# Keys and values of a cross-attention layer projected first, as seven block products, with attention by head group behind them

## The chip, the cores and the metric

The kernel runs on one core of a Trainium2 chip. The metric is the device time of one execution in microseconds; before the change the median of three runs was 1871.52 us (1866.82 to 1872.19).

## The reference

```python
x = x + tanh(g_xattn) * attn(layernorm(x), ctx)      # x: 8 x 100 x 1024, ctx: 8 x 361 x 1024
x = x + tanh(g_ffn) * experts(layernorm(x))
# attn(latents, context): 32 heads in 8 groups of 4, head size 128
kv = concatenate([context, latents])                 # 461 rows for each of 8 batches
q = rms_norm(latents @ Wq) * q_norm_w                # 1024 x 4096
k = rms_norm(kv @ Wk) * k_norm_w;  v = kv @ Wv       # each 1024 x 1024
out = softmax(q @ k.T / sqrt(128)) @ v, then @ Wo    # 4096 x 1024
# experts: 8 of rank 16, two chosen for each row
```

## The kernel before

Every large product is made to fp32 accuracy by splitting both operands into a rounded part (hi, written by ScalarE) and the rest (lo, subtracted by VectorE); `three` then issues hi times hi, hi times lo and lo times hi.

The order of the work is one hand-written program for each engine, tied together by semaphores; all DMAs are issued by SyncE.

1. Latents are normalised, transposed and split. Queries: 32 heads in two halves of 400 columns, 24 matmuls of 128x400 each. Their squares are summed over the head by TensorE (L615, L616: two matmuls of 128x400 for each half head), the sums turned by eight transposes for each group (L622), scaled by VectorE and raised to the power -0.5 by GpSimd (`group_rms`, L547). Queries go to internal DRAM.
2. Sixteen stages, one for each half of the key and value heads and each batch, with four slots. In a slot TensorE projects one tile of keys and values of the next stage (`proj_chunk`, 48 matmuls of 128x512: 8 blocks of the hidden size, keys and values, three each; a tile has 121, 120, 120 or 100 rows) and, between these, attention for one unit of four heads: `turn_keys`, `scores`, and for the unit before `turn_probs` and `values`. VectorE takes the maximum (L1351), the negated scale and the reciprocal, and multiplies the probabilities (`scale`, L1363); ScalarE takes the exponential (L1039). The key norm's power is on GpSimd (`key_rms`).
3. The output projection in 32 chunks of 4 heads, `chunk_head` being 12 matmuls of 128x400. The first eight run in the last stage beside attention (from 1470 us). From 1586 us on only the other 24 run, and then the small expert layer.

Where an instruction waits, all behind it on its engine wait too. The probabilities of a unit are turned after the next unit's first scores:

```python
scores(u, 0)                      # waits for kT_lo_done, q_lo_done
turn_probs(u - 1, par, t)         # t == 0 waits for p_done, 4 * u + 4 of that unit
```

## Time and profile before

| | us |
|---|---|
| time, median of 3 runs | 1871.52 |
| span of the profiled execution | 1867.1 |
| TensorE busy | 1803.3 (97%) |
| VectorE busy | 1099.9 (59%) |
| ScalarE busy | 846.7 (45%) |
| GpSimd busy | 152.0 (8%) |
| moved by DMA | 169.76 MB, 91 GB/s |

The profile gives the span from first to last instruction of one execution. Its own time outside that span is not shown; the span is 4.4 us under the median. Durations of matmuls overlap, since one starts before the other has drained: what a matmul costs a busy TensorE is the distance from its start to the next start. Busy time counts overlapping instructions once.

### The profile page before, as it was taken

The numbers are of one execution on the slowest core, as the hardware profiler recorded it, in microseconds if no ns is written. First come the engines' busy times: TensorE is split into PE (matmuls) and PEld (weight loads), VectorE is DVE, ScalarE is ACT, GpSimd is POOL, SyncE is SP. The second block draws the span as 40 slices with busy tenths as digits, with TensorE's granted clock in tenths as the row PEclk, the third lists the DMA queues.
The fourth block names the chain that finished last, engine by engine and source line by source line (L and its number), as shares of the span: only waits on it lengthen the run. The fifth ranks groups of instructions, "written<-read, shape, count | busy, mean of one in ns | idle before, by whom it ended". The sixth has DMA issues, their size and how long they took to land.

```text
span 1867.1 us, 26857 instructions
## 1 busy us (share of the span) xinstructions
PE 1803.3 (97%) x9512; PEld 1597.7 (86%) x9512; DVE 1099.9 (59%) x2308; ACT 846.7 (45%) x1594; POOL 152.0 (8%) x176
## 2 busy tenths in 40 slices
PE   5999999999999999999899999999999899999996
PEld 4999999878888888888688888888888789999994
DVE  6533333246666666666766666666666576455556
ACT  4433333235455555555655555554554455433321
POOL 3012111210000000000000000000000000000000
PEclk9999999999999999999999999999999999999999
DMA  6522232301111111111311111111111244656522
GB/s 208 184 99 80 84 133 80 121 21 57 40 57 46 50 56 37 59 52 41 107 57 53 44 57 39 56 56 39 56 41 63 98 178 166 237 186 222 212 98 62
DMA packets 62825, 169.76 MB, mean 91 GB/s; under 512 B 5808, under 2 KB 38576, under 8 KB 57616
## 3 DMA queue, kind: packets, MB, share of 16 engines
q1 hardware_dynamic: 62736, 168.69, 26.9%
q8 instruction: 42, 0.69, 0.2%
q14 instruction: 47, 0.39, 0.1%
HBM read 135.90 MB, written 32.77 MB: 90 GB/s over the span
## 4 chain that ended last, share of the span: by engine, by line
PE 91%; DVE 5%; ACT 2%; issue 1%; DMA 1%; POOL 0%; DVEq 0%; SPq 0%; ACTq 0%
PE bank L579 27%; PE bank L580 27%; PE bank L581 27%; PE bank L724 5%; PE bank L701 1%; PE bank L888 1%; PE bank L616 1%; PE bank L615 1%; DVE wo_lo L1328 0%; DMA w_raw<-Wkv 0%; ACT wo_hi L1016 0%; DMA xa<-x 0%; PE bank L622 0%; DVE at_lo L1333 0%; DVE w_lo L1237 0%
## 5 line engine op out<-in xcount | busy, mean ns | idle before, releaser
L579 PE MATMUL bank<-w_hi,kv_hi 128*128 128x512 f32 x1024 | 422.7, 413 | 2.6 <-DVE w_lo L1237 2.6
L580 PE MATMUL bank<-w_lo,kv_hi 128*128 128x512 f32 x1024 | 403.7, 394 | 0.0
L581 PE MATMUL bank<-w_hi,kv_lo 128*128 128x512 f32 x1024 | 403.7, 394 | 0.0
L1039 ACT ACTIVATE pr<-bank,nm,rqs 100x461 f32<-100x461 f32 x256 | 188.9, 738 | 417.8 <-DVE nm L1356 417.7
L1345 DVE TENSOR_TENSOR pT_lo<-bank,pT_hi 121x400 fp32r<-121x400 f32 x252 | 144.1, 572 | 169.5 <-ACT pT_hi L1032 169.5
L581 PEld LDWEIGHTS bank<-w_hi,kv_lo 128*128 128x128 f32 x1024 | 192.5, 188 | 44.2
L1351 DVE TENSOR_REDUCE mx<-bank 100x1 f32<-100x461 f32 x256 | 162.3, 634 | 114.9 <-PE bank L581 110.9
L579 PEld LDWEIGHTS bank<-w_hi,kv_hi 128*128 128x128 f32 x1024 | 193.1, 189 | 32.4 <-issue 1.7
L580 PEld LDWEIGHTS bank<-w_lo,kv_hi 128*128 128x128 f32 x1024 | 193.4, 189 | 29.9
L579 PE MATMUL bank<-at_hi,wo_hi 128*128 128x400 f32 x512 | 183.0, 357 | 9.2 <-DVE at_lo L1333 6.5
L579 PE MATMUL bank<-xT_hi,wq_hi 128*128 128x400 f32 x512 | 178.0, 348 | 2.4 <-DVE xT_lo L1212 2.4
L581 PE MATMUL bank<-at_hi,wo_lo 128*128 128x400 f32 x512 | 178.6, 349 | 0.0
L580 PE MATMUL bank<-at_lo,wo_hi 128*128 128x400 f32 x512 | 178.6, 349 | 0.0
L580 PE MATMUL bank<-xT_lo,wq_hi 128*128 128x400 f32 x512 | 177.7, 347 | 0.0
L581 PE MATMUL bank<-xT_hi,wq_lo 128*128 128x400 f32 x512 | 177.0, 346 | 0.0
L1032 ACT ACTIVATE pT_hi<-bank 121x400 fp32r<-121x400 f32 x252 | 125.3, 498 | 75.2 <-PE bank L724 75.2
L1264 DVE TENSOR_TENSOR sq_lo<-sq,sq_hi 128x400 fp32r<-128x400 f32 x64 | 36.8, 575 | 172.0 <-ACT sq_hi L980 172.0
L724 PE MATMUL bank<-ident,pr 100*120 100x100 f32 (+2 forms) x1024 | 134.5, 253 | 0.0
L724 PEld LDWEIGHTS bank<-ident,pr 100*120 100x120 f32 (+2 forms) x1024 | 116.8, 147 | 15.2
L1363 DVE TENSOR_SCALAR pr<-pr,rr 100x461 f32<-100x461 f32 x256 | 117.9, 461 | 9.1
L976 ACT ACTIVATE sq<-bank 128x400 f32<-128x400 f32 x64 | 32.3, 505 | 198.6 <-PE bank L581 198.6
L1328 DVE TENSOR_TENSOR wo_lo<-wo_raw,wo_hi 128x2048 fp32r<-128x2048 f32 x32 | 73.1, 2284 | 63.9 <-ACT wo_hi L1016 63.5
(128 smaller groups left out, 3059.6 us busy)
## 6 DMA issues: line engine op xcount, KB each, us to landing
wo_raw<-Wo SPq DMA_DIRECT2D x32, 1024.0 KB, 4.9
at_raw<-at_d SPq DMA_DIRECT2D x32, 800.0 KB, 6.8
wq_raw<-Wq SPq DMA_DIRECT2D x32, 512.0 KB, 6.6
kv_raw<-ctxT SPq DMA_DIRECT2D x32, 480.0 KB, 3.6
q_d<-qo SPq DMA_DIRECT2D x8, 1600.0 KB, 6.2
q_raw<-q_d SPq DMA_DIRECT2D x64, 200.0 KB, 2.4
at_d<-ao SPq DMA_DIRECT2D x64, 200.0 KB, 1.9
kv_raw<-ctxT SPq DMA_DIRECT2D x16, 484.0 KB, 3.6
```

Source lines behind the costliest of these rows:

```text
L579: pe.matmul(o, lh, rh, start=start, stop=False)
L580: pe.matmul(o, lh, rl, start=False, stop=False)
L581: return pe.matmul(o, ll, rh, start=False, stop=stop)
L724: mm = pe.transpose(ps[ptbank(t, last)][0:ROWS[t], i * NQ:(i + 1) * NQ], pr[0:NQ, par, i, OFF[t]:OFF[t] + ROWS[t]], ident[0:NQ, 0:NQ])
L976: act.activation(sq[:], ps[2 * (i % 2) + th][:, 0:TW], ACT.Square).then_inc(sq_done, 1)
L1032: act.activation(pT_hi[0:ROWS[t], t], ps[ptbank(t, not project)][0:ROWS[t], 0:QW], ACT.Copy).then_inc(pT_hi_done, 1)
L1039: act.activation(pr[0:NQ, j % 2, i], ps[sbank(i, not project)][0:NQ, 0:NK], ACT.Exp, bias=nm[0:NQ, i:i + 1], scale=rqs[0:NQ, i:i + 1], acc ...
L1264: dve.tensor_tensor(sq_lo[:, th], sq[:], sq_hi[:], ALU.subtract).then_inc(sq_lo_done, 1)
L1328: dve.tensor_tensor(wo_lo[:, k], wo_raw[k][:], wo_hi[:, k], ALU.subtract).then_inc(wo_lo_done, 1)
L1345: dve.tensor_tensor(pT_lo[0:ROWS[t], t], ps[ptbank(t, not project)][0:ROWS[t], 0:QW], pT_hi[0:ROWS[t], t], ALU.subtract).then_inc(pT_lo_do ...
L1351: dve.tensor_reduce(mx[0:NQ, i:i + 1], ps[sbank(i, not project)][0:NQ, 0:NK], AX.X, ALU.max).then_inc(mx_done, 1)
L1363: dve.tensor_scalar(pr[0:NQ, j % 2, i], pr[0:NQ, j % 2, i], rr[0:NQ, i:i + 1], None, ALU.mult).then_inc(p_done, 1)
```

## The change

Keys and values of all batches come first. The rows of four batches (4 x 461 = 1844) are packed into 15 tiles, and the two halves of the batches, the two halves of the hidden size and the pair keys and values make a product of 2x2 blocks, computed as seven block products (`P1` to `P7`) in Strassen's manner: 30 steps (`STEPS`, 15 tiles by two halves of the heads) of seven products with 12 matmuls of 128x512. The sums of inputs are made by GpSimd, the sums of weights by VectorE (first half) and GpSimd (second), the sums of results partly in the bank (`CHAIN`) and partly by VectorE in `cb`. Each step's keys are normalised, turned, split and stored to internal DRAM, as are the values; one buffer `kst` and one `vst` serve all stores. The latents' transposes are spread over eight steps (`X0`).

Then come nine parts of the queries' projection (a part is a half head, `AHEAD`), 55 slots of one attention unit and one part each, with the queries kept in SBUF, and nine slots with the remaining units, in the last eight of which 28 heads of the output projection run. The squares of a query part are summed by eight matmuls with the squares as the stationary operand and two columns of ones. Probabilities are scaled by GpSimd; loops are written out. From the end of the last unit on the program does what it did.

```diff
-                    mm = three(ps[BV if isv else BK][:, 0:KW], kv_hi[:, j, c], kv_lo[:, j, c],
-                               w_hi[:, c, isv * KW:(isv + 1) * KW], w_lo[:, c, isv * KW:(isv + 1) * KW],
-                               c == 0, c == C - 1)
...
-                    dve.tensor_scalar(pr[0:NQ, j % 2, i], pr[0:NQ, j % 2, i], rr[0:NQ, i:i + 1], None,
-                                      ALU.mult).then_inc(p_done, 1)
...
+ROWS_M = TB * NK
+CTX_M = TB * NC
+NT = -(-ROWS_M // P)
+STEPS = HALVES * NT
+MIXED = CTX_M // P
+KC = C // 2
+P1, P2, P6, P5, P7, P3, P4 = range(7)
+RING = 5
+W_ORDER = (P1, P2, P5, P7, P6, P3, P4)
+W_RANK = {o: n for n, o in enumerate(W_ORDER)}
+X0 = 2
+UNITS = G * B
+AHEAD = 9
+QB = 2 * R
+LAST_Q = UNITS - AHEAD
+OUT0 = LAST_Q
+HEADS_AT = {OUT0 + 1 + n: c for n, c in enumerate((3, 3, 4, 3, 4, 3, 4, 4))}
...
+        kT_d = nc.dram_tensor("kT_d", [P, G, 2, 2 * ROWS_M], F32).ap()
+        v_d = nc.dram_tensor("v_d", [2 * ROWS_M, G, 2, HD], F32).ap()
...
+        def a_src(k, o):
+            raw = kvr[:, k % 2]
+            n = cols(k % NT)
+            return {P1: raw[:, 0, 0:KC, 0:n], P2: raw[:, 0, KC:C, 0:n], P4: raw[:, 1, KC:C, 0:n],
+                    P6: st[:, 1, :, 0:n], P5: st[:, 0, :, 0:n], P7: st[:, 2, :, 0:n], P3: st[:, 1, :, 0:n]}[o]
+        def w_src(n):
+            return wr[:, (0, 1, 0, 2, 0, 3, 1)[n]]
...
     @block.sync
...
+            def store_k(k, m):
+                sp.wait_ge(kT_lo_done, 2 * k + m + 1)
+                h, r0, n = k // NT, rows_at(k, m), cols(k % NT)
+                sp.dma_start(kT_d[:, GH * h:GH * h + GH, :, r0:r0 + n].rearrange("p g l r -> p (g l) r"),
+                             kst[:].rearrange("p g l r -> p (g l) r")[:, :, 0:n].bitcast(F32)).then_inc(k_stored, 16)
+            def store_v(k, m):
+                sp.wait_ge(v_lo_done, 2 * k + 2 - m)
+                h, r0, n = k // NT, rows_at(k, m), cols(k % NT)
+                sp.dma_start(v_d[r0:r0 + n, GH * h:GH * h + GH], vst[0:n].bitcast(F32)).then_inc(v_stored, 16)
...
+            sp.dma_start(wr[:, 0], Wkv[0, 0]).then_inc(wr_in[0], 16)
+            load_kv(0)
+            for i in range(1, 4):
+                sp.dma_start(wr[:, i], Wkv[0, i]).then_inc(wr_in[i], 16)
+            sp.dma_start(qkw[:], vecs).then_inc(consts_in, 16)
+            sp.dma_start(rowc[:], rows).then_inc(consts_in, 16)
+            load_kv(1)
...
+                if k + 2 < STEPS:
+                    load_kv(k + 2)
...
+                store_k(k, 0)
...
+                store_v(k, 1)
+            store_v(STEPS - 1, 0)
+            store_k(STEPS - 1, 1)
...
     @block.gpsimd
...
+            def sums(k):
...
+                raw = kvr[:, k % 2, :, :, 0:n]
+                pool.wait_ge(kv_in[k % 2], kv_need(k))
+                if k >= 1:
+                    pool.wait_ge(a_lo_done, 7 * (k - 1) + P5 + 1)
+                pool.tensor_tensor(st[:, 0, :, 0:n], raw[:, 1, 0:KC], raw[:, 1, KC:C], ALU.add).then_inc(s_sum, 1)
+                pool.wait_ge(s_sum, 4 * k + 1)
+                if k >= 1:
+                    pool.wait_ge(a_lo_done, 7 * (k - 1) + P3 + 1)
+                pool.tensor_tensor(st[:, 1, :, 0:n], st[:, 0, :, 0:n], raw[:, 0, 0:KC], ALU.subtract).then_inc(s_sum, 1)
+                pool.tensor_tensor(st[:, 2, :, 0:n], raw[:, 0, 0:KC], raw[:, 1, 0:KC], ALU.subtract).then_inc(s_sum, 1)
+            def last_sum(k):
+                n = cols(k % NT)
+                pool.wait_ge(a_lo_done, 7 * k + P6 + 1)
+                pool.tensor_tensor(st[:, 1, :, 0:n], kvr[:, k % 2, 0, KC:C, 0:n], st[:, 1, :, 0:n],
+                                   ALU.subtract).then_inc(s_sum, 1)
...
+            sums(0)
+            last_sum(0)
+            for k in range(STEPS):
+                if k >= 1:
+                    key_rms(k - 1, 1)
+                if k == NT:
+                    weight_sums(3)
+                if k + 1 < STEPS:
+                    sums(k + 1)
+                if 0 <= k - X0 < B:
+                    latent_rstd(k - X0)
+                if k == NT - 1:
+                    weight_sums(0)
+                key_rms(k, 0)
+                if k == NT - 1:
+                    weight_sums(1)
+                if k + 1 < STEPS:
+                    last_sum(k + 1)
+                if k == NT - 1:
+                    weight_sums(2)
+            key_rms(STEPS - 1, 1)
+            def group_rms(g):
+                pool.wait_ge(ms_done, g + 1)
+                pool.tensor_tensor(rq[0:NQ, g], ms[0:NQ], mhalf[0:NQ], ALU.pow).then_inc(rq_done, 1)
+            def scale(u, i):
+                a = 4 * u + i
+                pool.wait_ge(rr_done, a + 1)
+                pool.tensor_scalar(pr[0:NQ, u % 2, i], pr[0:NQ, u % 2, i], rr[0:NQ, i:i + 1], None,
+                                   ALU.mult).then_inc(p_done, 1)
+            group_rms(0)
+            for u in range(UNITS):
+                for i in range(R):
+                    scale(u, i)
+                    if u % B == B - 1 and i == 0 and u + 1 < UNITS:
+                        group_rms(u // B + 1)
...
     @block.tensor
...
+            def product(k, o, bank, start):
+                h, n, p = k // NT, cols(k % NT), 7 * k + o
+                pe.wait_ge(a_lo_done, p + 1)
+                if k % NT == 0:
+                    pe.wait_ge(w_lo_done, 7 * h + W_RANK[o] + 1)
+                s = p % RING
+                for c in range(KC):
+                    mm = three(ps[bank][0:n, 0:KW], a_hi[:, s, c, 0:n], a_lo[:, s, c, 0:n], w_hi[:, o, c], w_lo[:, o, c],
+                               start and c == 0, c == KC - 1, not start)
+                mm.then_inc(prod_done, 1)
...
+            def step(k):
+                a = CHAIN[k % 2]
+                if k >= 2:
+                    pe.wait_ge(kn_done, 2 * (k - 2) + 2)
+                product(k, P1, a, True)
+                if k >= 1:
+                    pe.wait_ge(c12_done, k)
+                product(k, P2, BK, True)
+                if k >= 1:
+                    turn_keys(k - 1, 1)
+                pe.wait_ge(p1_done, k + 1)
+                product(k, P6, a, False)
+                if k >= 1:
+                    pe.wait_ge(c22_done, k)
+                    pe.wait_ge(c12a_done, k)
+                product(k, P5, CK, True)
+                pe.wait_ge(u2_done, k + 1)
+                product(k, P7, a, False)
+                turn_keys(k, 0)
+                pe.wait_ge(c11_done, k + 1)
+                product(k, P3, BK, True)
+                if 0 <= k - X0 < B:
+                    turn_latents(k - X0)
+                pe.wait_ge(u3_done, k + 1)
+                product(k, P4, a, False)
...
+            def squares(n):
+                g, i, th = n // QB, n // 2 % R, n % 2
+                pe.wait_ge(sq_lo_done, n + 1)
+                if n == 0:
+                    pe.wait_ge(ones_done, 1)
+                    pe.wait_ge(kT_lo_done, 2 * STEPS - 1)
+                if n % QB == 0 and g >= 1:
+                    pe.wait_ge(ms_done, g)
+                for bb in range(TB):
+                    c0 = 2 * (R * (TB * th + bb) + i)
+                    o = ps[SS][0:NQ, c0:c0 + 2]
+                    pe.matmul(o, sq_hi[:, bb * NQ:(bb + 1) * NQ], ones[:], start=True, stop=False)
+                    mm = pe.matmul(o, sq_lo[:, bb * NQ:(bb + 1) * NQ], ones[:], start=False, stop=True)
+                mm.then_inc(ss_done, 1)
...
+            for n in range(AHEAD):
+                for c in range(C):
+                    query_part(n, c)
+                    if n == 0 and c == 1:
+                        turn_keys(STEPS - 1, 1)
+                    if n >= 1 and c == 4:
+                        squares(n - 1)
...
+            def slot(u):
+                n = u + AHEAD if u < LAST_Q else None
+                def c_(c):
+                    if n is not None:
+                        query_part(n, c)
+                scores(u, 0)
+                if u >= 1:
+                    turn_probs(u - 1, 0)
+                c_(0)
+                scores(u, 1)
+                if u >= 1:
+                    turn_probs(u - 1, 1)
+                c_(1)
...
+                c_(3)
+                if u >= 1:
+                    values(u - 1, 2)
+                c_(4)
+                if u + AHEAD - 1 < 2 * H:
+                    squares(u + AHEAD - 1)
+                c_(5)
+                if u >= 1:
+                    values(u - 1, 3)
+                c_(6)
+                c_(7)
...
     @block.scalar
...
+            def values_hi(k, m):
+                v, n = 2 * k + 1 - m, cols(k % NT)
+                if v >= 1:
+                    act.wait_ge(v_stored, 16 * v)
+                act.activation(vst[0:n, :, 0], cb[0:n, 1 + m].rearrange("p (g d) -> p g d", g=GH), ACT.Copy).then_inc(v_hi_done, 1)
...
     @block.vector
...
+            weight_lo(0, 0)
+            operand_lo(0)
+            dve.wait_ge(wr_in[2], 16)
+            weight_sum(0, 2, 0)
+            weight_lo(0, 1)
+            operand_lo(1)
+            dve.wait_ge(wr_in[3], 16)
+            dve.wait_ge(t_done, 1)
+            weight_sum(2, 3, 2)
+            weight_lo(0, 2)
+            dve.wait_ge(w_lo_done, 3)
+            weight_sum(0, 3, 0)
+            operand_lo(2)
+            weight_lo(0, 3)
+            operand_lo(3)
+            weight_lo(0, 4)
+            dve.wait_ge(t_done, 3)
+            weight_sum(1, 1, 0)
...
+            def at_product(k, o):
+                if k == 0 and o == 0:
+                    weight_lo(0, 5)
+                if k == 0 and o == 2:
+                    weight_lo(0, 6)
+                if (k, o) in W_AT:
+                    weight_lo(1, W_AT[k, o])
+                p = 7 * k + o + RING - 1
+                if o == 0 and k >= 1:
+                    key_sums(k - 1, 1)
+                if o == 1 and k >= 1:
+                    normalise_keys(k - 1, 1)
+                if o == 2:
+                    sum_c11(k)
+                if o == 5:
+                    sum_c22(k)
+                    start_c12(k)
+                if o == 6:
+                    sum_c12(k)
+                if o == 4:
+                    normalise_keys(k, 0)
+                if p < 7 * STEPS:
+                    operand_lo(p)
+                if o == 0 and k >= 1:
+                    values_lo(k - 1, 0)
...
+            def mean_squares(g):
+                dve.wait_ge(ss_done, QB * g + QB)
+                if g >= 1:
+                    dve.wait_ge(rq_done, g)
+                dve.tensor_scalar(ms[0:NQ].rearrange("p (n o) -> p n o", o=1),
+                                  ps[SS][0:NQ, 0:2 * B * R].rearrange("p (n o) -> p n o", o=2)[:, :, 0:1],
+                                  1.0 / HD, RMS_EPS, ALU.mult, ALU.add).then_inc(ms_done, 1)
...
+            def slot(u):
+                n = u + AHEAD - 1
+                prev = u >= 1
+                maxima(u, 0)
+                if prev:
+                    p_split(u - 1, 0)
...
+                    p_split(u - 1, 3)
+                inverse(u, 3)
+                if u % B == B - 1 and u + 1 < UNITS:
+                    mean_squares(u // B + 1)
+                if u + 1 < UNITS:
+                    q_split(u + 1)
+                if n < 2 * H:
+                    next_wq(n)
```

## Rows read from the trace of the kernel before

**Rows 1.** the profile's page: engine busy time, and last chain by engine

```profile
PE 1803.3 (97%) x9512; PEld 1597.7 (86%) x9512; DVE 1099.9 (59%) x2308; ACT 846.7 (45%) x1594; POOL 152.0 (8%) x176
...
PE 91%; DVE 5%; ACT 2%; issue 1%; DMA 1%; POOL 0%; DVEq 0%; SPq 0%; ACTq 0%
```

**Rows 2.** stretches of the span: length, busy time of each engine, clock, DMA

```profile
0.00:42.00 42.00, 18.74 (x97) 16.03 (x98) 29.34 (x56) 18.46 (x30) 15.81 (x24) 0.99 0.61 198
...
1470.00:1586.00 116.00, 105.75 (x589) 100.32 (x588) 77.42 (x126) 58.67 (x87) 0.00 (x0) 0.97 0.47 171
1586.00:1867.10 281.10, 260.58 (x1452) 246.96 (x1450) 152.84 (x222) 91.25 (x87) 13.65 (x16) 0.99 0.48 170
```

**Rows 3.** matmuls in order of time, 128x512: start, duration; first and last of 104

```profile
370.72 0.39 PE L580 MATMUL bank<-w_lo,kv_hi 128*128 128x512 f32 x1
...
394.64 0.40 PE L581 MATMUL bank<-w_hi,kv_lo 128*128 128x512 f32 x1
```

**Rows 4.** the last chain in order of time: one period of the queries' loop

```profile
132.63 0.87 PE bank L622 x8
171.42 0.87 PE bank L622 x8
```

**Rows 5.** the last chain in order of time: four key and four probability transposes

```profile
410.27 0.40 PE bank L701 x4
410.68 0.42 PE bank L724 x4
```

**Rows 6.** matmuls in order of time: scores; first of one head and what follows

```profile
903.67 0.37 PE L579 MATMUL bank<-kT_hi,q_hi 128*100 128x462 f32 x1
...
904.30 0.34 PE L579 MATMUL bank<-pT_hi,v_hi 120*128 120x400 f32 x1
```

**Rows 7.** groups by form: count, busy, mean ns of one

```profile
L1431 DVE TENSOR_TENSOR v_lo<-v_raw,v_hi 128x512 fp32r<-128x512 f32 x64 | 43.8, 685 | 0.5 <-ACT v_hi L1103 0.5
...
L1351 DVE TENSOR_REDUCE mx<-bank 100x1 f32<-100x461 f32 x256 | 162.3, 634 | 114.9 <-PE bank L581 110.9
...
L1039 ACT ACTIVATE pr<-bank,nm,rqs 100x461 f32<-100x461 f32 x256 | 188.9, 738 | 417.8 <-DVE nm L1356 417.7
...
L1363 DVE TENSOR_SCALAR pr<-pr,rr 100x461 f32<-100x461 f32 x256 | 117.9, 461 | 9.1
...
L1328 DVE TENSOR_TENSOR wo_lo<-wo_raw,wo_hi 128x2048 fp32r<-128x2048 f32 x32 | 73.1, 2284 | 63.9 <-ACT wo_hi L1016 63.5
...
L1016 ACT ACTIVATE wo_hi<-wo_raw 128x2048 fp32r<-128x2048 f32 x32 | 61.3, 1916 | 108.5 <-PE bank L581 100.9 <-DMA at_raw<-at_d 7.6
```

**Rows 8.** GpSimd and VectorE in order of time, around a group's mean squares

```profile
101.60 5.44 POOL L547 TENSOR_TENSOR rqt<-ms,mhalf 100x32 f32<-100x32 f32 x1 [66.58 <-DVE ms L1249]
...
104.96 0.57 DVE L1264 TENSOR_TENSOR sq_lo<-sq,sq_hi 128x400 fp32r<-128x400 f32 x1 [3.44 <-ACT sq_hi L980]
```

**Rows 9.** GpSimd and VectorE in order of time, in the output projection

```profile
1671.98 2.24 DVE L1328 TENSOR_TENSOR wo_lo<-wo_raw,wo_hi 128x2048 fp32r<-128x2048 f32 x1
...
1672.15 2.12 POOL L570 TENSOR_SCALAR mv<-mv 100x1 f32<-100x1 f32 x1 [205.77 <-DVE mv L1473]
```

**Rows 10.** GpSimd in order of time, at the start

```profile
1.28 0.29 POOL L535 TENSOR_SCALAR_AFFINE_SELECT ident<-ident 128x128 f32<-128x128 f32 x1 [0.24 <-POOL epst L533]
```

**Rows 11.** DMA issues by line: size, median us to landing

```profile
wo_raw<-Wo SPq DMA_DIRECT2D x32, 1024.0 KB, 4.9
...
kv_raw<-ctxT SPq DMA_DIRECT2D x32, 480.0 KB, 3.6
...
at_d<-ao SPq DMA_DIRECT2D x64, 200.0 KB, 1.9
```

**Rows 12.** matmuls in order of time, after a wait in the last slots

```profile
1478.02 0.67 PE L579 MATMUL bank<-at_hi,wo_hi 128*128 128x400 f32 x1 [3.62 <-DVE at_lo L1333]
1478.49 0.54 PE L580 MATMUL bank<-at_lo,wo_hi 128*128 128x400 f32 x1
1478.82 0.54 PE L581 MATMUL bank<-at_hi,wo_lo 128*128 128x400 f32 x1
```

More of the change, by code:

```diff
@@ new lines, in _ @@
+            sums(0)
+            last_sum(0)
+            for k in range(STEPS):
+                if k >= 1:
[15 more added lines that the diff above has]
+                    weight_sums(2)
@@ L594, in _, with three @@
-            pe.wait_ge(pool_consts, 4)
-            for b in range(B):
+            def three(o, lh, ll, rh, rl, start, stop, more=False):
+                pe.matmul(o, lh, rh, start=start, stop=False, skip_group_check=more)
+                pe.matmul(o, lh, rl, start=False, stop=False, skip_group_check=more)
+                return pe.matmul(o, ll, rh, start=False, stop=stop, skip_group_check=more)
+            def product(k, o, bank, start):
[8 more added lines that the diff above has]
+                mm.then_inc(prod_done, 1)
@@ L903, in _ @@
             accumulators_free(0, 1)
-            chunk(0, 1, 0, 0, first=True)
-            chunk(0, 1, 0, 1)
-            with pe.Fori(1, G // 2 - 1) as gp:
-                chunk(0, 1, gp, 0)
-                chunk(0, 1, gp, 1)
-            chunk(0, 1, G // 2 - 1, 0)
-            chunk(0, 1, G // 2 - 1, 1, last=True)
+            for m in range(G, 2 * G):
+                chunk(m)
             for c in range(2 * G):
@@ new lines, in _, with p_split @@
+            ins.then_inc(pad_done, 1)
+            for n in range(AHEAD - 1):
+                copy_queries(n)
+                squares_lo(n)
+                next_wq(n)
+            mean_squares(0)
+            q_split(0)
+            def p_split(u, t):
+                dve.wait_ge(pT_hi_done, 4 * u + t + 1)
+                if t == 0 and u >= 1:
+                    dve.wait_ge(pv_done, u)
+                dve.tensor_tensor(pT_lo[0:ROWS[t], t], ps[ptbank(u, t)][0:ROWS[t], 0:QW],
+                                  pT_hi[0:ROWS[t], t], ALU.subtract).then_inc(pT_lo_done, 1)
@@ L1435, in _ @@
-            for j in range(KT):
-                slot(-1, j, 1, 0, False, True)
-                if j == 0:
-                    mean_squares(G)
-                if j == 2:
-                    keep_rms(G)
-            q_split(0)
-            normalise_keys(0, 0, 0)
-            stages(dve, lambda s, par, half: [slot(s, j, par, half, True, projects(s)) for j in range(GH)])
-            last = 4 * STAGES - 1
+                dve.tensor_tensor(at_lo[:, m % 2], at_raw[:, m % 2], at_hi[:, m % 2], ALU.subtract).then_inc(wo_lo_done, 1)
```

1835 lines of the change are left out of this document (875 added, 960 removed).

## The prediction

> **What bounds the kernel now.** I read the page first: TensorE is busy for 1803.3 of 1867.1 us and makes up 91% of the chain that ended last; VectorE has 59%, ScalarE 45%, GpSimd 8% [rows 1]. Then the stretches, to see where TensorE is idle: 42 − 18.74 = 23.3 us in the first 42 us, 116 − 105.75 = 10.3 us in the last stage beside the output projection, 20.5 us in the 281.1 us after 1586 us [rows 2]. The whole span has 1867.1 − 1803.3 = 63.8 us idle [rows 1], so 43.3 us lie ahead of 1586 us, where all edits are. What comes after is the same program and is kept at 281.1 us. Last the lists in order of time, for what one matmul costs a full queue. Durations mislead there, since they overlap. From 370.72 to 394.64 us there are 103 steps from start to start: 0.2322 us for a 128x512 [rows 3], though its duration is 0.39. A queries' group lasts 38.79 us with 208 matmuls of 128x400 and eight transposes of 0.87 together [rows 4]: 0.1823 us each. Four transposes take 0.40 [rows 5], the three matmuls of a scores' head 904.30 − 903.67 = 0.63 [rows 6].
>
> **What TensorE issues less or more.** (a) Projection: 1024 x 3 = 3072 matmuls become 30 steps x 7 x 12 = 2520 of the same 128x512 form (the tile of 52 rows only has fewer columns in the stationary operand). 552 x 0.2322 = −128.2 us [rows 3]. (b) Squares: 128 matmuls of 128x400 go, −23.3 us [rows 4]; 512 with two moving columns and 100 stationary ones come. No row has this form. A small transpose also has a short stream behind a full load of the stationary operand: 0.87/8 = 0.109 us [rows 4]; the cheapest is 0.35/4 to 0.40/4 [rows 5]; the dear end is a full 0.1823. I take 0.109: +55.7, net +32.4 (bounds +22 and +70). (c) The turned sums go: eight times 0.87, −7.0 us [rows 4]. (d) Key transposes: 64 x 4 become 60 x 4, −0.4 x 4 = −1.6 us [rows 5]. Queries, scores, values, probabilities and output keep their counts. Sum: −104.4 us of work for TensorE. In return it waits where it did not.
>
> **The start.** The first step needs all seven weight blocks. A load of 1024 KB lands after 4.9 us and one of 480 KB after 3.6 [rows 11], so each further MB adds 1.3/544 x 1024 = 2.4 us. The first 1 MB, issued at 0.8, lands at 5.7 and, with tile 0 between, the third weight load at 5.7 + 3 x 2.4 = 13 us. VectorE stands at it, with the second block's lo queued behind; from there seven operations of 2048 columns at 2.28 and three of 512 at 0.69 lie ahead of the third product [rows 7], which starts at 13 + 16 + 2 = 31 us. Behind it come the last weight, two more, and the first key norm (square, sum, power, product) before the sixth product; the step ends near 50 us against 20.4 for a full one: 30 us idle, where the start had 23.3.
>
> **The other 29 steps.** A step is 84 x 0.2322 + 0.9 = 20.4 us for TensorE. VectorE has 19 operations of 512 columns at 0.69, 13 us [rows 7]; it hides if no wait falls wrong. The closest is the one buffer for values: `values_hi` waits for the store before it. That store can start some 0.2 us before the step's end; its 512 KB take between 1.9 (200 KB) and 3.6 to 3.8 us [rows 11]. Then ScalarE and VectorE run 0.63 + 0.69, and the product that normalises the second key block is queued behind, 0.69: done 5.5 us into the next step, when `turn_keys` is due after two products of 2.79. So it nearly hides; the GpSimd sums can push it. I take 0.4 us for each step, 12 us (0 to 60).
>
> **Second half's weights.** Seven subtractions, 16 us of VectorE, and four GpSimd sums of 2048 columns fall on steps 14 and 15. The sums are bounded by VectorE's 2.28 [rows 7] and 16 x 0.29 = 4.6 [rows 10], scaled by columns from 128. The key sums queue behind the subtractions; I take 14 us (4 to 30). **Handover** to the queries: last key norm, 6.5 MB of split latents and the first group's power before the first exponential, 8 us (3 to 15).
>
> **The slots.** A slot: 24 x 0.1823 + 4 x 0.63 + 12 x 0.1823 + 1.5 + 0.9 = 11.5 us, where there were 17.9. VectorE and ScalarE have about 8.5 and 8 us. Fourth scores end 6.6 us into the slot; maximum 0.63 and exponential 0.74 [rows 7], two operations on one column and the reading of the accumulator between them, and the queue ahead of them (the fourth head's own split among it) lead to about 9.3; GpSimd's fourth scaling follows. It is due at 11.5 + 0.6 = 12.1. Bounds for one scaling: VectorE's 0.46 [rows 7] and 0.29 x 461/128 = 1.04 [rows 10]; I take 0.9, nearer the GpSimd row. It hides with 1.9 us to spare, and the slots cost nothing more.
>
> **Group boundaries.** Not hidden. GpSimd raises 32 columns to the power in 5.44 us [rows 8]. Before, that lay beside the queries with nothing behind. Now, in each eighth unit, it is queued after the first scaling and waits for `mean_squares`, which VectorE does only after the fourth reciprocal, at 9.4. So power until 15, three scalings until 17.7, and `turn_probs` due at 12.1 waits 5.5 us. After 3.62 us of idle, matmuls of 128x400 came 0.33 us apart instead of 0.18, which is 1.2 GHz instead of 2.4 (the stretch's granted clock is 0.97) [rows 2, 12]; some ten of them so spaced cost 1.5 us. Six boundaries at 7 us, and one in unit 55, whose slot has no queries to cover it, at 11: 53 us (35 to 65).
>
> **Last slots.** Their wait before was 10.3 us in four slots [rows 2], from weights and heads split behind attention (1.9 + 2.3 us for the weights alone [rows 7]). Eight such slots: 19 us (10 to 35).
>
> **Sum.** New idle 30 + 12 + 14 + 8 + 53 + 19 = 136 us, old 43.3. −104.4 + 136 − 43.3 = −11.7, so a span of 1855.4. The median lies 1871.5 − 1867.1 = 4.4 above the span of before: **1860 us**.
>
> **Rows against a rule.** A GpSimd operation on one element, issued 0.17 us into VectorE's 2.24 us subtraction, took 2.12 us and ended just after it [rows 9]. But VectorE's 0.57 us subtraction ran at its usual length inside GpSimd's 5.44 us power [rows 8]. The Trainium skill (SBUF — State Buffer, section "SBUF: two separate sides") says that the two engines share a port pair which one holds for a whole instruction while the other fully blocks. By that the first row agrees and the second does not; for sums that stream rather than compute no row here decides. The Trainium skill (GPSIMD Engine Reference, section 3.1 on elementwise work) gives 4497 ns for a GpSimd addition of 2048 columns; by it one sum of 512 would be an estimated 1.1 us, against 1.16 by scaling the row.
>
> **Rivals.**
> *R1, boundaries hidden, TensorE stays the bound.* The 53 us vanish if the power is shorter than 5.4 or the profile's VectorE runs ahead; with steps unstalled too: 1860 − 53 − 20 (steps, weights) = 1787. For: TensorE has been 97% busy in a program of the same kind [rows 1]. Against: the order of GpSimd's queue. Chance 0.17.
> *R2, slower: GpSimd's scaling is late in each slot.* It decides from 3 us for the fourth scaling, less if those before wait. VectorE's next subtractions, 0.57 and in every second slot 1.22, may go first, as in the wait of [rows 9]. Each 1 us late costs 62 us over the units: 1922. Chance 0.17.
> *R3, slower: VectorE and GpSimd exclude each other in the steps.* GpSimd has four sums at 1.16 and two powers at 1.2, 7 us, on top of VectorE's 13: 20 of 20.4, and more in the eight steps with latents. If nothing overlaps, order leaves some 2 us for each step and the weights cost 15 more: 1860 + 50 + 15 = 1925. Chance 0.16. This is what the Trainium skill's port rule (SBUF — State Buffer, same section) would do here.
> *The forecast,* 0.5, own range 1825 to 1885.
>
> A difference within 0.3% (5.6 us) can't be told from none. The forecast's half splits into 0.36 faster, 0.10 same, 0.04 slower: faster 0.36 + 0.17 = 0.53; same 0.10; slower 0.04 + 0.17 + 0.16 = 0.37. The range runs from R1 to beyond R2 and R3: 1775 to 1935.
>
> **What would show it.** 2520 matmuls 0.232 apart; the two-column squares 0.11 apart; one step every 20.4 to 21.3 us; the third product at about 31 us; slots of 11.5 to 12; TensorE idle over 4 us only at units 8, 16 to 56, waiting for GpSimd's scaling; 136 + 20.5 = 157 us of idle in all against 63.8. Wrong if steps exceed 22 us, slots exceed 12.3, or the two-column squares cost 0.18.

## The result, and the profile after

The changed kernel takes **1986.55 us** (median of 4 runs, 1984.04 to 1988.65), the kernel before 1871.76 (4 runs, 1866.82 to 1872.19): a ratio of 1.0617, 95% interval 1.0601 to 1.0633. It is 6.2% slower, outside the range of 1775 to 1935.

The page of the changed kernel, profiled at a span of 1983.7 us:

```profile
PE 1748.3 (88%) x9264; PEld 1542.6 (78%) x9264; DVE 1174.7 (59%) x2129; ACT 913.5 (46%) x1680; POOL 713.4 (36%) x548
...
PEclk8998988889999998999989998999897899999998
...
DMA packets 229494, 278.12 MB, mean 140 GB/s; under 512 B 67972, under 2 KB 203972, under 8 KB 223732
...
PE 68%; DMA 11%; DVE 8%; POOL 5%; issue 3%; ACT 3%; SPq 1%; DVEq 0%; ACTq 0%; POOLq 0%
PE bank L654 20%; PE bank L655 19%; PE bank L656 19%; DMA v_d<-vst 7%; PE bank L778 5%; POOL rq L631 2%; DMA kT_d<-kst 2%; POOL pr L636 2%; PE bank L675 2%; PE bank L745 1%; DVE a_lo L1291 1%; PE bank L744 1%; DVE wo_lo L1524 1%; DVE kn L1315 1%; DVE w_lo L1297 1%
```

Against [rows 1], TensorE's share of the last chain fell from 91% to 68%, and DMA went from 1% to 11%: 7% of the span is the store of values. TensorE is idle for 1983.7 − 1748.3 = 235.4 us, where the prediction had 156.5, and busy for 1748.3, where it had 1803.3 − 104.4 = 1698.9. The two differences, 78.9 and 49.4, are the 128.3 us between the predicted span of 1855.4 and this one.

Where it was lost is seen by cutting the span at the work's own marks: the issue of a step's first key store (steps 0, 15, 29), the first scores, the end of TensorE's work ahead of unit 55's first scores, the first copy of an accumulator.

```profile
0.00:51.09 51.09, 25.33 (x78) 19.32 (x79) 39.33 (x30) 22.67 (x24) 19.59 (x18) 0.83 0.37 144
51.09:464.00 412.91, 335.77 (x1443) 266.86 (x1442) 240.25 (x333) 160.87 (x272) 153.43 (x141) 0.89 0.68 152
464.00:748.52 284.52, 281.39 (x1287) 226.12 (x1286) 177.98 (x265) 127.67 (x224) 109.69 (x109) 1.00 0.61 154
748.52:816.55 68.03, 52.79 (x302) 49.95 (x299) 18.27 (x30) 14.22 (x24) 2.47 (x3) 0.87 0.49 158
816.55:1502.20 685.65, 638.20 (x3933) 595.58 (x3931) 452.11 (x1073) 413.64 (x901) 355.11 (x227) 0.96 0.36 109
1502.20:1696.30 194.10, 151.45 (x780) 135.62 (x780) 93.83 (x177) 83.14 (x149) 59.40 (x37) 0.87 0.45 151
1696.30:1983.70 287.40, 263.36 (x1451) 249.18 (x1450) 152.91 (x222) 91.26 (x87) 13.68 (x16) 0.97 0.49 171
```

(Length, then busy time of TensorE, its loads, VectorE, ScalarE and GpSimd, the granted clock, the DMA share and GB/s.) Beside the prediction's terms:

| stretch | predicted | after | more |
|---|---|---|---|
| step 0 | 50 | 51.1 | +1 |
| steps 1 to 15: 15 x 20.8 + 14 | 326 | 412.9 | **+87** |
| steps 16 to 29: 14 x 20.8 | 291 | 284.5 | −7 |
| way to the first scores: 216 x 0.1823, 64 x 0.109, rest of a step 4, idle 8 | 59 | 68.0 | +9 |
| units 0 to 54: 55 x 11.5 + 42 | 675 | 685.7 | +11 |
| units 55 to 63 (what is left of 1855) | 173 | 194.1 | +21 |
| output | 281 | 287.4 | +6 |

Steps 16 to 29 took 20.3 us each at full clock, as forecast; the same program took 27.5 us in steps 1 to 15, at 0.89. Of the 87 us more, 60 lie in steps 1 to 10 (267.9 us for 208), 15 in steps 11 to 13, 12 in the last two. What ScalarE does in step 4, in order of time:

```profile
147.12 12.65 SPq L380 DMA_DIRECT2D v_d<-vst  x2
...
158.06 0.63 ACT L1014 ACTIVATE vst<-cb 128x512 fp32r<-128x512 f32 x1 [8.41 <-DMA v_d<-vst]
158.72 0.69 DVE L1329 TENSOR_TENSOR vst<-cb,vst 128x512 fp32r<-128x512 f32 x1 [8.28 <-ACT vst L1014]
159.33 0.69 DVE L1315 TENSOR_TENSOR kn<-bank,rk 128x512 f32<-128x512 f32 x1
...
160.07 1.12 PE L675 MATMUL bank<-ident,kn 128*128 128x128 f32 x4 [6.14 <-DVE kn L1315]
```

The first value store of the step is issued at 147.12, and the next split of values can begin only at 158.06: the store took 10.9 us to land, and ScalarE, VectorE and TensorE stood behind it in turn, 8.41, 8.28 and 6.14 us. In step 16 the same chain runs so:

```profile
486.50 4.57 SPq L380 DMA_DIRECT2D v_d<-vst  x2
489.35 0.63 ACT L1014 ACTIVATE vst<-cb 128x512 fp32r<-128x512 f32 x1 [1.09 <-DMA v_d<-vst]
490.02 0.69 DVE L1329 TENSOR_TENSOR vst<-cb,vst 128x512 fp32r<-128x512 f32 x1 [0.95 <-ACT vst L1014]
490.62 0.68 DVE L1315 TENSOR_TENSOR kn<-bank,rk 128x512 f32<-128x512 f32 x1
...
492.39 0.60 PE L675 MATMUL bank<-ident,kn 128*128 128x128 f32 x4
```

Here it landed in 2.85 us, and TensorE didn't wait; in steps 16 to 29 it had two waits over 0.4 us, of 1.1 and 0.9. Over the whole program, by the list of waits (total, times, longest):

```profile
ACT vst L1014 <- DMA v_d<-vst: 120.8, 29, 12.5
...
PE bank L675 <- DVE kn L1315: 88.8, 23, 11.3
```

A boundary between groups (unit 7 to 8):

```profile
906.38 0.19 DVE L1468 TENSOR_SCALAR ms<-bank 100x32 f32<-100x32 f32 x1 [0.68 <-PE bank L745]
906.65 5.71 POOL L631 TENSOR_TENSOR rq<-ms,mhalf 100x32 f32<-100x32 f32 x1 [4.25 <-DVE ms L1468]
912.36 4.29 POOL L636 TENSOR_SCALAR pr<-pr,rr 100x461 f32<-100x461 f32 x3
...
916.70 1.14 PE L778 MATMUL bank<-ident,pr 100*121 100x100 f32 x4 [7.41 <-POOL pr L636]
```

This is the queue that was forecast: power, then three scalings, then TensorE. Each scaling takes 1.43 us, not 0.9. From store to store of attention's outputs a slot is 11.37 us, and the six at boundaries are 21.0, 21.8, 20.7, 21.7, 20.6 and 21.7: 9.9 more each, where I had 7.

At unit 55 the prediction had one wait, for the power. It is there, and ahead of it stands another:

```profile
1502.24 0.36 SPq L478 DMA_DIRECT2D wo_raw<-Wo  x1
...
1503.67 0.60 SPq L479 DMA_DIRECT2D at_raw<-at_d  x1
1504.31 0.53 SPq L452 DMA_DIRECT2D kT<-kT_d  x1
...
1515.28 0.70 PE L654 MATMUL bank<-kT,q_hi 128*100 128x462 f32 x1 [13.07 <-DMA kT<-kT_d]
...
1528.46 5.71 POOL L631 TENSOR_TENSOR rq<-ms,mhalf 100x32 f32<-100x32 f32 x1 [6.84 <-DVE ms L1468]
...
1534.16 4.29 POOL L636 TENSOR_SCALAR pr<-pr,rr 100x461 f32<-100x461 f32 x3
...
1538.50 1.14 PE L778 MATMUL bank<-ident,pr 100*121 100x100 f32 x4 [7.81 <-POOL pr L636]
```

SyncE waits for the last query (1502.2) before the output's first two chunks, 3.6 MB, and the load of unit 55's keys stands behind them: 13 us. The power and three scalings then hold TensorE for 7.81 us, as at the other boundaries.

### The profile page after: what moved, and what is told of

It is laid out like the page before. It is cut to its first block, busy times and chain, and to the rows that moved or that the text cites. A ratio compares the mean times of both kernels' runs of the same rounds, so it can differ in the third digit from the quotient of the medians.

```text
span 1983.7 us, 26304 instructions
## 1 busy us (share of the span) xinstructions
PE 1748.3 (88%) x9264; PEld 1542.6 (78%) x9264; DVE 1174.7 (59%) x2129; ACT 913.5 (46%) x1680; POOL 713.4 (36%) x548
## 4 chain that ended last, share of the span: by engine, by line
PE 68%; DMA 11%; DVE 8%; POOL 5%; issue 3%; ACT 3%; SPq 1%; DVEq 0%; ACTq 0%; POOLq 0%
PE bank L654 20%; PE bank L655 19%; PE bank L656 19%; DMA v_d<-vst 7%; PE bank L778 5%; POOL rq L631 2%; DMA kT_d<-kst 2%; POOL pr L636 2%; PE bank L675 2%; PE bank L745 1%; DVE a_lo L1291 1%; PE bank L744 1%; DVE wo_lo L1524 1%; DVE kn L1315 1%; DVE w_lo L1297 1%
## 5 line engine op out<-in xcount | busy, mean ns | idle before, releaser
L636 POOL TENSOR_SCALAR pr<-pr,rr 100x461 f32<-100x461 f32 x256 | 370.2, 1452 | 420.5 <-DVE rr L1520 420.5
L654 PE MATMUL bank<-w_hi,a_hi 128*128 128x512 f32 (+1 forms) x840 | 347.5, 414 | 28.5 <-DVE a_lo L1291 13.9
L655 PE MATMUL bank<-w_lo,a_hi 128*128 128x512 f32 (+1 forms) x840 | 338.9, 403 | 0.0
L656 PE MATMUL bank<-w_hi,a_lo 128*128 128x512 f32 (+1 forms) x840 | 338.1, 403 | 0.0
L1153 ACT ACTIVATE pr<-bank,nm,rq 100x461 f32<-100x461 f32 x256 | 188.7, 737 | 147.2 <-DVE nm L1511 144.4
L654 PEld LDWEIGHTS bank<-w_hi,a_hi 128*128 128x128 f32 (+1 forms) x840 | 162.1, 193 | 67.0 <-issue 21.5
L1144 ACT ACTIVATE pT_hi<-bank 120x400 fp32r<-120x400 f32 (+2 forms) x256 | 129.1, 504 | 144.9 <-PE bank L778 144.9
L1499 DVE TENSOR_TENSOR pT_lo<-bank,pT_hi 120x400 fp32r<-120x400 f32 (+2 forms) x256 | 145.2, 567 | 83.8 <-ACT pT_hi L1144 81.9
L656 PEld LDWEIGHTS bank<-w_hi,a_lo 128*128 128x128 f32 (+1 forms) x840 | 161.1, 192 | 40.5 <-issue 0.6
L778 PE MATMUL bank<-ident,pr 100*120 100x100 f32 (+2 forms) x1024 | 141.9, 262 | 55.7 <-POOL pr L636 55.7
L655 PEld LDWEIGHTS bank<-w_lo,a_hi 128*128 128x128 f32 (+1 forms) x840 | 162.1, 193 | 36.6 <-issue 0.4
```

What stands on the lines that cost most here:

```text
L636: pool.tensor_scalar(pr[0:NQ, u % 2, i], pr[0:NQ, u % 2, i], rr[0:NQ, i:i + 1], None, ALU.mult).then_inc(p_done, 1)
L654: pe.matmul(o, lh, rh, start=start, stop=False, skip_group_check=more)
L655: pe.matmul(o, lh, rl, start=False, stop=False, skip_group_check=more)
L656: return pe.matmul(o, ll, rh, start=False, stop=stop, skip_group_check=more)
L778: mm = pe.transpose(ps[ptbank(u, t)][0:ROWS[t], i * NQ:(i + 1) * NQ], pr[0:NQ, u % 2, i, OFF[t]:OFF[t] + ROWS[t]], ident[0:NQ, 0:NQ])
L1144: act.activation(pT_hi[0:ROWS[t], t], ps[ptbank(u, t)][0:ROWS[t], 0:QW], ACT.Copy).then_inc(pT_hi_done, 1)
```

## Experiments

Each is the changed kernel with one edit, unless it says otherwise. Kernels were run in four sessions, each on one chip: e1 to e4; e0, e5, e6, e8; e10, e11; e12, e13. All but e10 are single runs, beside which the kernel before took 1868.2 to 1872.0 us. "Steps 1 to 10" is a ninth of the time between the first key stores of steps 1 and 10; it was 27.5 us in the changed kernel. Line numbers are each kernel's own.

**e1: the power in two halves.** Of a group's squares only the last part belongs to the second half of the batches, so the first 16 columns can be raised a slot earlier.

```diff
-                    if u % B == B - 1 and i == 0 and u + 1 < UNITS:
-                        group_rms(u // B + 1)
+                if u % B >= B - 2 and u // B + 1 < G:          # behind the fourth scaling
+                    group_rms(u // B + 1, u % B - B + 2)       # 16 of 32 columns
```

> Only the group boundaries are changed: the 32 columns raised to the power on GpSimd become two halves of 16 columns, the first in the last unit but one of a group, the second in the last unit, each queued after the unit's fourth scaling. Theory (the boundary is GpSimd's queue order: the 5.7 us power ahead of three scalings of 1.43 us): a half takes about 2.9 us, every slot of units 0 to 53 takes 11.4 us, the six of 20.6 to 21.8 us are gone (6 x 9.9 = 59 us), the wait of 7.8 us at unit 55 and some 3 us ahead of the first exponential go too: 1986 - 67 = about 1919 us. Rival (a power costs about the same whatever its columns, or the reciprocals themselves are late at a boundary): boundaries of 16 us and more remain, 1950 us or above.

Measured 1898.78 us. All slots to unit 53 take 11.4 us; a half takes 2.93 us, or 3.72 beside VectorE's 1.23 us split of the queries' weights. The boundaries' 59 us are gone, and unit 56 fell from 25.8 to 20.9. The gain of 88 us is more than was forecast, but 13 of it lie in steps 1 to 15, which the edit doesn't touch (below, e0); 3 more lie from there to the first scores, 7 in the first and the last units. The theory stands.

**e2: the power behind the fourth scaling**, one instruction moved (`i == R - 1` for `i == 0`).

> Only one instruction moves: at a boundary GpSimd's power over 32 columns is queued after the fourth scaling, not after the first. Theory (the three scalings wait behind the power): the turned probabilities no longer wait; the power ends some 6 us later than the boundary's last scaling and the first exponential of the next group waits for it, so that a boundary costs 3 to 5 us in place of 9.9: 1986 - 36 = about 1950 us. Rival (what costs is the length of the power wherever it stands): boundaries stay at 20 to 22 us and the time at 1980 or more.

Measured 1929.01 us. A boundary takes 15.8 us, so it costs 4.4 in place of 9.9, 33 us less in all; of the other 24, 11 are again in the steps, 5 between them and the first scores and 5 in unit 56. So 5.5 us of a boundary were three scalings waiting behind a power that nobody yet needed, and 4.4 the power itself.

**e3: the split latents stored in large pieces.**

```diff
-        xh_d = nc.dram_tensor("xh_d", [P, 2, C, TW], F32).ap()
+        xh_d = nc.dram_tensor("xh_d", [P, 2, TB, C, NQ], F32).ap()    # xl_d and both in SBUF the same
```

> The split latents (two of the three stores of a latent tile) go to memory in pieces of 3200 bytes instead of 400; the same bytes, and the queries read them in another order. Theory A (the value store lands late because 3 x 1024 small pieces of each latent tile stand ahead of it and keep the DMA engines busy): their landing falls from 10 to 11 us to about 5, steps 2 to 10 fall from some 29 us to 23 to 25: 1986 - 40 = about 1946 us. Rival B (the bytes count, 4.6 MB for each of these steps, not the pieces): steps stay at 27 to 29 us and the time at 1975 or more.

Measured 1962.75 us, with steps 1 to 10 at 24.3 us where e1 and e2 of the same session had 26.3 and 26.5: 2.1 us less a step, theory A in kind, at about half its size. The two stores land in 7.4 and 7.2 us instead of 8.9 and 10.0 in e1. The first scores came at 780.7 us, in e1 and e2 at 800.4 and 800.8; but 11 us were lost behind them. The queries' matmuls, which now read their 400 columns as four runs of 100, came 0.1853 us apart and not 0.1823, a slot took 11.48 us and a boundary 22.0. e10 and e12 have the same layout, and slots of 11.47 and 11.48 us.

**e4: two buffers for the split values.**

```diff
+            return v % 2 if 1 <= k <= X0 + B or k > NT else 0     # the second lies in free weight space
...
-                    act.wait_ge(v_stored, 16 * v)
+                    act.wait_ge(v_stored[s], v_before(v, s))
```

> A second staging buffer for the split values, used in steps 1 to 10 and from step 16 on; a value store then has a whole product more to land in. Theory A (the round trip of one buffer is what stalls ScalarE, then VectorE, then the turning of the keys): ScalarE's wait for the store, 120.8 us in 29 times, nearly vanishes outside steps 11 to 15, steps 2 to 10 fall from some 29 us to 20.4 to 22.5, the 12.5 us wait ahead of the queries goes too: 1986 - 75 = about 1911 us. Rival B (the DMA engines cannot move the 4.6 MB of a latent step in 20 us): the steps stay at 26 us or more, the wait moves to the context's load or the key store: 1986 - 25 = about 1961 us.

Measured 1916.98 us. Steps 1 to 10 take 21.65 us, the store of step 15 is issued at 404.9 us instead of 451 to 453 in e1 and e2, the first scores come at 746.9 us instead of 800.4 and 800.8, and ScalarE's wait for value stores fell from 120.8 to 17.8 us. Part of it became a wait for key stores, 45.7 us between 90 and 330 us where the changed kernel had 2.5, as rival B had foreseen, but the steps were short all the same. The stretch from 71 to 265 us in the changed kernel, in e3 and in e4:

```profile
71.00:265.00 194.00, 161.44 (x714) 131.90 (x713) 110.56 (x171) 76.03 (x135) 67.13 (x71) 0.90 0.77 164
```

```profile
71.00:265.00 194.00, 176.09 (x786) 143.04 (x785) 122.42 (x189) 84.27 (x149) 75.63 (x80) 0.94 0.67 184
```

```profile
71.00:265.00 194.00, 188.21 (x894) 153.77 (x893) 138.79 (x212) 94.20 (x169) 83.44 (x89) 1.00 0.90 207
```

The DMA engines were at a share of 0.77 while TensorE waited for them, and with the second buffer they moved 207 GB/s instead of 164 (175 in e1). So throughput did not bind: one buffer's round trip did. But at 0.90 little was left. e3 needed 0.67 for 184 GB/s, e4 0.90 for 207: with the small pieces the stretch's traffic takes 19% more engine time for a byte. e10 below has two buffers and large pieces, and needs 0.81 for 222, e3's ratio.

**e11: the latents' stores on ScalarE's own queue**, with one value buffer and small pieces.

> The three stores of a latent tile are issued by ScalarE on its own queue, not by SyncE ahead of the context's load, the key store and the value store; the same bytes in the same small pieces, one value buffer. Theory A (the value store is late because it stands behind them in one queue): it overtakes them, ScalarE's wait for it falls from 120 to some 70 us, steps 2 to 10 fall from 29 to 24 us or less: about 1945 us. Rival B (the 16 DMA engines are shared by all queues, so that order matters little and the load on them does): steps stay at 28 us or more, 1975 us or above, and ScalarE, which now issues three DMAs a step, may add to it.

Measured 1954.72 us, between the two. Steps 1 to 10 take 25.5 us, 0.9 less than in e1 and e2, and the third latent store lands after 15.0 us instead of 10.0 in e1. No unaltered kernel ran beside it; against e1 and e2, whose context loads landed in 7.8 us as here, the store of step 15 came 13 us earlier (438.9), where the second buffer gave 47. The same step in e1 and here:

```profile
144.05 12.19 SPq L380 DMA_DIRECT2D v_d<-vst  x2
154.53 0.63 ACT L1018 ACTIVATE vst<-cb 128x512 fp32r<-128x512 f32 x1 [7.93 <-DMA v_d<-vst]
```

```profile
142.89 0.69 ACT L992 ACTIVATE kst<-bank,wqk 128x512 fp32r<-128x512 f32 x1 [3.03 <-DMA kT_d<-kst]
...
146.19 9.26 SPq L380 DMA_DIRECT2D v_d<-vst  x2
153.75 0.63 ACT L1004 ACTIVATE vst<-cb 128x512 fp32r<-128x512 f32 x1 [7.20 <-DMA v_d<-vst]
```

In steps 3 to 8 the value store lands in 3.5 to 7.6 us, in e1 and e2 in 8.8 to 10.5: it overtakes the latents, as A says. But a step's second key store, which stood ahead of the latents before, now lands in 5.4 to 10.0 us instead of 4.8 to 5.3 (steps 2 to 9), and ScalarE waits for key stores for 18.4 us between 90 and 330 us where e1 had 0.7. So order in the queue is a large part of the value store's landing, and changing it alone moves the wait. The Trainium skill (DMA: Bandwidth & Descriptors, "Issuing engines are not separate DMA queues") says that DMAs of all engines run on the same 16 DMA engines and interleave; that the other stores slow down agrees.

**e8: one weight block a step**, two in step 11, one each in steps 12 and 13.

> The second half's 4 MB of weights, issued together in step 11 ahead of the stores, are issued as two blocks in step 11 and one in each of steps 12 and 13. Theory (one queue in order: 4 MB hold the value store back by some 20 us): steps 11 and 12, 27.4 and 30.5 us (25 and 30 in the other runs), fall to 21 to 24 us, 1986 - 10 = about 1976 us. Rival (the loads only fill gaps; steps 11 and 12 are long for the load of the last context tile and the latents in small pieces): within 3 us of the unaltered kernel in the same call.

Measured 1980.46 us; steps 11 and 12 together 50.9 us, 58.2 in the unaltered kernel of the same session (e0, 1987.36); e5 and e6, whose edits don't touch these steps, had 55.7 and 57.5. So some 5 to 7 us were the 4 MB ahead of the value store.

**e5: the second half's weight sums on VectorE.**

```diff
-                if k == NT - 1:
-                    weight_sums(0)        # and three more, on GpSimd
...
+                        weight_sum(to, x, y)    # on VectorE, behind each of the first four weight_lo
```

> The four sums of weight blocks for the second half move from GpSimd (4.5 to 5.1 us each) to VectorE (2.3 us each). Theory (the two engines exclude each other while a sum of the one and a two-input operation on SBUF of the other run: a 52x512 operation of VectorE took 5.09 us beside a 5.06 us sum): in place of 4 x 4.8 = 19 us in which VectorE stands still, 9 us of its own work: steps 14 and 15, 34 and 33 us, fall by 7 to 10 us together, 1986 - 8 = about 1977 us. Rival (GpSimd's sums run beside VectorE's work, which is the bound in these steps): VectorE has 9 us more to do and the two steps grow by 5 to 9 us, 1993 us.

Measured 1976.01 us; steps 14 and 15 together 59.3 us instead of 67.5 in e0. VectorE was given 9 us more work, and the two steps fell by 8 (the whole by 11, of which 2.5 lie in steps 11 and 12, ahead of the edit). In the changed kernel, in order of time:

```profile
431.67 5.06 POOL L601 TENSOR_TENSOR wr<-wr 128x2048 f32<-128x2048 f32 x1
...
432.19 5.09 DVE L1329 TENSOR_TENSOR vst<-cb,vst 52x512 fp32r<-52x512 f32 x1
...
443.64 4.53 POOL L605 TENSOR_TENSOR wr<-wr 128x2048 f32<-128x2048 f32 x1
...
444.30 5.65 DVE L1291 TENSOR_TENSOR a_lo<-st,a_hi 128x512 fp32r<-128x512 f32 x1
```

Operations of VectorE that take 0.68 us alone lasted until GpSimd's sum was over and 0.5 us more; the second also spans a short sum of 1.27 us issued at 448.14. They and a third, 5.96 us where 2.28 is usual, cost VectorE 13 us: the engines do exclude each other. e5 alone doesn't show that this is the gain, since it also takes the long sums out of GpSimd's queue, for which ScalarE's split of the weights waited 3.4 to 5.3 us, three times. The Trainium skill (SBUF — State Buffer, "Who interferes with whom") says that a VectorE instruction with two inputs in SBUF contends with a GpSimd instruction that reads SBUF, and that one with at most one, outside the two-port modes, does not. The trace agrees: of the additions with one input in PSUM (second group below) 36 began inside a sum of GpSimd, at least 0.3 us before its end, and none took over 0.69 us; of those with two inputs in SBUF (first group) 7 did, and their median is 1.19 us.

```profile
L1291 DVE TENSOR_TENSOR a_lo<-st,a_hi 128x512 fp32r<-128x512 f32 x112 | 85.2, 761 | 4.4 <-ACT a_hi L970 3.7
L1334 DVE TENSOR_TENSOR cb<-bank,cb 128x512 f32<-128x512 f32 x112 | 74.2, 683 | 20.7 <-ACT cb L1035 17.5 <-PE bank L656 2.4
```

**e6: unit 55's keys ahead of the chunks**, on top of e1; the two `load_chunk` calls and their wait move behind `load_vv(u + 1)`.

> Power in halves as in e1, and the loads of unit 55's keys and values are issued ahead of the wait for the last query and of the output's first two chunks, not behind them. Theory (TensorE's 13.1 us wait for keys at unit 55 is SyncE's order alone): unit 55, 26.0 us, falls to 15 to 17 us, and what the chunk loads then hold back is hidden: e1's 1898.8 - 10 = about 1889 us. Rival (the next wait, for the chunks' weights or for the heads' split, takes its place): no more than 3 us gained, 1896 us or above.

Measured 1906.8 us, more than e1, yet units 54 and 55 took 11.4 and 16.2 us instead of 15.4 and 25.9: 13.7 us gained where the theory put them, with 2.7 us of wait for keys left. Its store of step 15 was issued at 465.1 us, in e1 at 450.7, and its first scores came at 820.1 us, in e1 at 800.4: the 20 us that it was behind there lie ahead of the edit, and outweigh the gain.

**e0 and e13: the changed kernel again.**

> The changed kernel unaltered, for the spread of its first half beside the runs of the same call: steps 1 to 15 took 413 us in its profile, but 400 to 402 us in the two experiments that touch only the attention. If that is the chip's or the memory's doing, this run lies anywhere from 1970 to 1988 us, with slots of 11.4 us and boundaries of 20.6 to 22 us as before; if not, 1984 to 1988 us.

> The changed kernel unaltered, on the same chip as the run beside it, since the first half of the steps differed by some 14 us between chips (store of step 15 issued at 451 to 453 us in e1 and e2, at 464 to 468 in the changed kernel's two profiles). If this chip is of the first kind: about 1973 us; if of the second: 1984 to 1988 us. Slots of 11.4 us and boundaries of 20.6 to 22 us either way.

Measured 1987.36 and 1989.26 us, the store of step 15 at 467.8 and 466.2, the slots at 11.4 as ever. e13 ran on the same chip as e1 and e2, which had 451 and 453; so it isn't the chip. It goes with how long a context load takes to land: 7.8 to 8.0 us in e1 to e4, e10 and e11, 8.6 to 8.9 in the others. What sets that, and whether it is the cause, is open. e0, e6 and e13, with the longer landing, issue the store of step 15 12 to 17 us later than e1 and e2.

**e10: all mended**: e1, e3, e4 (until step 11), e5, e6 and e8.

> The changed kernel with the power in halves (e1), large latent pieces (e3), two value buffers (e4, here until step 11), weight sums on VectorE (e5), unit 55's keys ahead of the chunks (e6) and weights one block a step (e8). Theory (the five waits are apart in time and their gains add): from 1987 us, 67 for the boundaries, 14 for unit 55, 8 for the weight sums, 7 for the weights' loads, 58 for steps 2 to 10 and the way to the queries, and some 5 more for the pieces: about 1828 us (1815 to 1840), faster than the kernel before. Rival (the waits cover each other: behind the one removed stands the next, the key store or GpSimd's sums): 1850 us or above, steps 2 to 10 at 22 us or more.

Measured **1811.70 us** (5 runs, 1809.45 to 1814.17) against 1868.19 for the kernel before (9 runs): a ratio of 0.9696, interval 0.9682 to 0.9709. Its page, and the stretch from 71 to 265 us:

```profile
span 1808.8 us, 26339 instructions
...
PE 1708.8 (94%) x9264; PEld 1516.2 (84%) x9264; DVE 1178.8 (65%) x2141; ACT 913.5 (51%) x1680; POOL 707.9 (39%) x552
```

```profile
71.00:265.00 194.00, 194.00 (x929) 160.71 (x928) 145.71 (x219) 98.33 (x175) 91.27 (x92) 1.00 0.81 222
```

TensorE doesn't stop in the latents' steps, which take 20.7 us. What is left over 20 us is mainly step 14 with 36.0 (VectorE's weight work) and step 15 with 22.9. The gains are apart in time and add. The 1828 expected started from 1987; from the 1973 that e1's and e2's first half stands for, it would have been 1814.

**e12: all mended but the second value buffer.**

> As the mended kernel (1811.7 us) but with the one value buffer of the changed kernel. Theory A (the single buffer is the stall, what else is in the queue only lengthens it): steps 1 to 10 take 24 to 25 us as with large pieces alone, and the way to the queries has its 11 us wait back: 1811.7 + 4 x 9 + 11 = about 1859 us. Rival B (with the pieces large and the weights spread the store lands in time): steps at 21.5 us or less, below 1830 us.

Measured 1877.82 us, 19 more than theory A had, with steps 1 to 10 at 25.5 us and ScalarE back to 105 us of waits for value stores: A in kind. Of the 66 us more, 56 lie ahead of the store of step 15, 6 in steps 16 to 29 and 4 on the way to the queries; up to 14 may be the session's (its context loads landed in 8.9 us, in e10 8.0). With all else mended, one more buffer of 4 KB for each partition is thus worth 52 to 66 us, and without it the kernel is not faster than the one before (1870.21 beside it).

## Why the prediction was wrong

**The step that failed** is "the other 29 steps": 0.4 us each, 12 us. It named the right mechanism, the round trip of the one value buffer, and its margin was right where it applied: in steps 16 to 29 the store landed in time and a step took 20.3 us. But in steps 1 to 10 a step took 27, over the 22 us that the prediction had set as a sign of being wrong. The store's duration was taken from a size alone, 3.6 to 3.8 us by [rows 11], which are landings in a kernel that moved 91 GB/s. In steps 2 to 10 the same SyncE queue carries, ahead of that store, three latent stores of 400 KB in 400-byte pieces, a latent load, 1 MB of context and the key store. It landed in 10.9 us, and e4 and e12 show that this was the stall. I had left the latents' traffic out; the 60 us of steps 1 to 10 are 47% of the error, and steps 1 to 15 together, 87 us, 68%. Of the 60, 44.3 are eight waits of TensorE for the second keys; the rest I did not trace, but the granted clock was 0.90 from 71 to 265 us. The bound that I gave, 60 us for all steps, was too near.

**The weights' term** (14 us, 4 to 30) measured 67.5 − 2 x 20.3 = 27 us in e0, the exclusion of rival R3 included, plus 5 to 7 us ahead of it for their load (e8), which had no term.

**Group boundaries**: the mechanism was right, GpSimd's queue with the power ahead of three scalings (e1, e2). Each cost 9.9 us, not 7: a scaling takes 1.43 us and not 0.9, above the upper bound of 1.04 that [rows 10] gave by columns, so the three add 1.6, and the power, 5.71 for 5.44, 0.3: TensorE's wait is 7.41 us, not 5.5. The last 1.0 is what a boundary costs beyond its wait, 2.5 us for 1.5; behind the wait matmuls come 0.33 us apart again, but that this is all of it I did not show.

**Unit 55**: the wait for the power was there, 7.81 us in its slot without queries; in e1 that unit is 4.9 us shorter. What had no term is SyncE's order, 13.07 us (e6). Without the two the last stretch is idle for 194.10 − 151.45 − 20.88 = 21.8 us, where **the last slots** had 19.

**The way to the queries** (8 us): 15.2 us idle, 11.3 of it one wait for the same value buffer, behind 6.5 MB of latents. It is at the bound of 15, from the same cause as in the steps; without it others take its place, and the way is only 3.3 us (e4 beside e1) or 4.3 (e10 beside e12) shorter.

**The output**, kept at 281.1 us, took 287.4 with as many matmuls (1451 for 1452): 3.5 us more idle and 2.8 more busy, at a granted clock of 0.97 for 0.99. Why is not traced.

**Right**: the third product at 32.5 us (31 predicted) and step 0; steps of 20.3 and slots of 11.37 us (20.4 and 11.5); the two-column squares 0.09 us apart (0.109, bounds not needed), seen here between two queries' matmuls:

```profile
905.56 0.16 PE L744 MATMUL bank<-ones,sq_hi 128*100 128x2 f32 x1
905.58 0.23 PE L745 MATMUL bank<-ones,sq_lo 128*100 128x2 f32 x1
905.67 0.23 PE L744 MATMUL bank<-ones,sq_hi 128*100 128x2 f32 x1
...
906.20 0.43 PE L654 MATMUL bank<-xT_hi,wq_hi 128*128 128x400 f32 x1
```

The work for TensorE was right within 1%: 1698.9 us predicted, 1708.8 in e10 at a granted clock of 0.98. That it was busy for 1748.3 in the changed kernel, with as many matmuls and a clock of 0.94, goes with the clock: after the wait of 5.51 us that ended at 444.44, nine matmuls of 128x512 came 0.43 us apart, not 0.23, which is 1.2 GHz (granted clock 0.52 from 444 to 450 us). I had charged that to the boundaries and to nothing else.

**The rivals.** R1 (boundaries hidden) is what e1 makes, but the unaltered kernel doesn't. R2 (the fourth scaling late in each slot) is wrong: at 1.45 us it is 60% dearer than I took it, and slots still take 11.37. R3 (the engines exclude each other) holds, and costs time in steps 14 and 15, where GpSimd's operation is long; a plain step still took 20.3 us, since its four sums of 1.37 to 1.72 us leave room: the sums that I priced at 1.16 took a third more, and hid. The sign was called faster at 0.53 against 0.37, with no rival for memory traffic at all, although the change moves 278 MB where 170 were moved.

## What to carry to other kernels

The same 512 KB landed in 2.85 us or in 10.9, by what was issued ahead of them: before a round trip is put beside a deadline, list what is issued ahead of it in that step, in bytes and in pieces. A second copy of a buffer whose store is waited for is the first thing to try; here it was worth 50 us and more. Before a store gets large pieces by another layout, look at who reads it back: here the reader's matmuls came 0.003 us further apart, and attention took 11 us more. And read each engine's queue past a long operation for who is next: moving one power behind three scalings was worth 5.5 us a time, and halving it to use the slot before removed the rest.
